# Pairs attention: two head groups worked as a pair, with 64-column quarters shared, and exponentials of three banks

## The chip, the core and the metric

The kernel runs on one core of one Trainium2 chip. The metric is the device time of one launch in microseconds, lower is better. Three timed runs of the kernel before gave 1415.05 us in the median (1402.74 to 1417.5). One more run was profiled; its own time is 1408.72 us and the span of its records is 1406.9 us.

## The reference

The program is a small vision tower: an embedding, and three layers with different attentions and feed-forward parts. The change is in the attention of the third layer's first half, called "pairs" in the kernel. It has 32 heads of width 2 over 1025 tokens, two batches, causal. Per head:

```python
q, k, v = split(x_normed @ w_qkv.T)            # heads of 2 values
q = rmsnorm(q) * qn_w ; k = rmsnorm(k) * kn_w
s = (q @ k.T) / sqrt(2)                        # causal: key <= query
y = softmax(s) @ v
x = x + y @ w_proj.T
```

The last token (number 1024) is treated apart, so the main loop works on 1024 tokens, which are 8 tiles of 128 keys by two halves of 512 queries.

## The kernel before, in words

`stage_pairs` is one stage of six. `pairs_prepare` (L2173) makes q, k and v; `pairs_attend` (L2334) does the attention; `pairs_project` (L2558) projects. In `pairs_attend`:

- Heads are worked four at a time. Two batches of 32 heads give `BH = 16` such head groups. The four heads of a group lie on partitions 0, 32, 64 and 96 (12 rows each, since q and k are split into bf16 parts that are multiplied exactly), so that their four score matmuls stand in different row strips of TensorE.
- A score block is 128 keys by 512 query columns of one head, one PSUM bank. The causal triangle makes 9 steps of four blocks (one per head) for each head group: `steps`. Step 0 is key tile 0 against queries 0 to 511; step 1 joins tile 1 (384 columns) with tile 3 (128 columns); step 2 joins 256 columns of the first query half with 256 of the second; steps 3 to 7 are whole tiles against queries 512 to 1023; step 8 joins tiles 5 and 7.
- TensorE computes the scores of a step (L2546), in two units of two banks each. PSUM has six banks for scores, so three units are in flight: a unit waits for the exponential of the unit three before it (`exp_ok`, `u - 2`).
- ScalarE exponentiates a unit (L2476), 128x1024 from PSUM into the ring `PT` in SBUF, which holds four steps.
- VectorE sets the part above the diagonal to zero (L2460): a multiplication with the triangle `keep` over 128 columns of four heads. That is 8 instructions for a head group: one in steps 0 and 7, two in steps 1, 2 and 8.
- TensorE then multiplies the weights with the values, in float32, two steps behind the scores (`attend(n - 2)`, L2512): four heads in four column strips, 32 columns of the array each, accumulating in PSUM bank 6. When a query half is complete, VectorE copies bank 6 to `Yc` (L2453, semaphore `y_sb`), and the first attend of the next half waits for that copy.
- Bank 7 is used by the "turns": four transposes that bring q or k of the next head group (L2501, copied by VectorE at L2418), and transposes that bring the result of the head group before back (L2492; L2406 and L2408 divide it). One turn stands behind each of steps 0 to 6.

TensorE's program is thus written by hand: for each step, scores, then the attend of two steps before, then a turn. All engines work in order. A wait in TensorE's program holds up all that stands behind it.

Of the kernel before, what the change touches and what calls it, by code (L numbers as in the profile page):

```python
# [21 lines left out]
D = 64  # L22
# [29 lines left out]
def constants():  # L52
# [48 lines left out]
    c["c_keep"] = np.triu(np.ones((128, 128), np.float32))  # L101
# [2056 lines left out]
def stage_pairs(nc, K, A):  # L2158
    with ExitStack() as ctx:
# [3 lines left out]
        V1 = sb("V1", [128, T, 128])  # L2163
        qk = sb("qk", [128, T, 128])
        wpT = sb("wpT", [64, 64])
        pairs_prepare(nc, K, A, Q12, K12, V1, qk, wpT)
        Yt = sb("Yt", [128, 16, 32, 2])
        YL = sb("YL", [1, 2, 32, 2])
        pairs_attend(nc, K, A, Q12, K12, V1, qk, Yt, YL)
# [3 lines left out]
def pairs_prepare(nc, K, A, Q12, K12, V1, qk, wpT):  # L2173

    with ExitStack() as ctx:
# [23 lines left out]
        with nc.Block() as block:  # L2199
# [7 lines left out]
            @block.gpsimd  # L2207
            def _(pool):
                nc.gpsimd.memset(zero[:], 0.0).then_inc(zero_ok, 1)
                nc.gpsimd.memset(V1[:], 1.0).then_inc(ones_ok, 1)  # L2210

# [101 lines left out]
            def _(pe):  # L2313
# [7 lines left out]
                for u in range(9):  # L2321
# [12 lines left out]
def pairs_attend(nc, K, A, Q12, K12, V1, qk, Yt, YL):  # L2334
# [3 lines left out]
    BH = 16  # L2338

    steps = [[(0, 0, 0, 0, 512)],  # L2340
             [(0, 1, 0, 128, 384), (0, 3, 384, 384, 128)],
             [(0, 2, 0, 256, 256), (1, 6, 256, 256, 256)]]
    steps += [[(1, j, 0, 0, 512)] for j in range(5)]
    steps += [[(1, 5, 0, 128, 384), (1, 7, 384, 384, 128)]]
    per = len(steps)
    diag = {0: (0,), 1: (0, 384), 2: (0, 256), 7: (0,), 8: (0, 384)}
    RING = 4
    N = BH * per

    TURNS = {0: ("q", 0), 1: ("q", 1), 2: ("k", 0), 3: ("k", 1), 4: ("y", 0), 5: ("y", 1), 6: ("y", 2)}  # L2350
    YTILES = ((0, 3), (3, 6), (6, 8))
    LAST_STEP = 4 * per + 8

    def turns_at(n):
        bh, s = n // per, n % per
        found = []
        if s in TURNS:
            which, i = TURNS[s]
            owner = bh - 1 if which == "y" else bh + 1
            if 0 <= owner < BH:  # L2360
                found.append((owner, which, i))
# [3 lines left out]

    FIRST = [(0, which, i) for which in "qk" for i in range(2)]
    number = {turn: k for k, turn in enumerate(FIRST + [turn for n in range(N + per) for turn in turns_at(n)])}
    masked = [0]
    for n in range(N):
        masked.append(masked[-1] + (n % per in diag))  # L2370
    with ExitStack() as ctx:
# [4 lines left out]
        keep = sb("keep", [128, 128])  # L2376
        QT = sb("QT", [128, 2, 1024], BF16)
        KT = sb("KT", [128, 2, 1024], BF16)
        PT = sb("PT", [128, RING, 4, 512])
# [8 lines left out]
        chain, ls_ok, le_ok, lw_ok = sem("chain"), sem("ls_ok"), sem("le_ok"), sem("lw_ok")  # L2388
        with nc.Block() as block:
            @block.sync  # L2390
            def _(sp):
                sp.dma_start(keep[:], A["c_keep"]).then_inc(c_in, 16)

            @block.vector
            def _(dve):
# [4 lines left out]
                def bring(bh, which, i):  # L2400
# [13 lines left out]
                    else:  # L2414
                        if bh >= 2:
                            dve.wait_ge(s_ps, 2 * per * (bh - 1))
                        dst = QT if which == "q" else KT
                        ins = nc.vector.tensor_copy(dst[:, bh % 2, 512 * i:512 * i + 512],  # L2418
                                                    ps[:, 7, :].bitcast(BF16)[:, 0:512])
# [21 lines left out]

                for t in FIRST:
                    bring(*t)
                dve.wait_ge(c_in, 16)
                for n in range(N + per):
                    bh, s = n // per, n % per
                    if n >= 2 and n - 2 < N and (n - 2) % per in (2, 8):
                        c = (n - 2) % per // 8
                        k = 2 * ((n - 2) // per) + c
                        dve.wait_ge(av_ps, n - 1)  # L2450
                        if k >= 4:
# [1281 lines left out]
```

## Time and profile before

| | |
|---|---|
| median of three runs | 1415.05 us (1402.74 to 1417.5) |
| profiled execution, its own time | 1408.72 us |
| its span | 1406.9 us |
| PE busy (matmuls) | 1082.8 us, 77% |
| DVE busy | 890.9 us, 63% |
| ACT busy | 764.2 us, 54% |
| POOL busy | 139.2 us, 10% |
| exponentials of the pairs attention (L2476) | 288, busy 266.1 us, first at 652.1, last start 919.4 |

PE is TensorE's matmul row, PEld its weight loads, DVE is VectorE, ACT ScalarE, POOL GpSimd. The stage that the change touches most lies between 646 and 926 us of the span. The rest of the kernel is the same before and after. A float32 matmul appears in the trace as two records (two passes), and so do its weight loads; a bf16 matmul is one record. The record of a matmul begins when it starts to stream and ends when the last result is out, so records of successive matmuls overlap. The time that TensorE needs for a piece of work is best read from the start of one group to the start of the next.

### The profile page before, as it was taken

The numbers are of one execution on the slowest core, as the hardware profiler recorded it, in microseconds if no ns is written. First come the engines' busy times: TensorE is split into PE (matmuls) and PEld (weight loads), VectorE is DVE, ScalarE is ACT, GpSimd is POOL, SyncE is SP. The second block draws the span as 40 slices with busy tenths as digits, with TensorE's granted clock in tenths as the row PEclk, the third lists the DMA queues.
The fourth block names the chain that finished last, engine by engine and source line by source line (L and its number), as shares of the span: only waits on it lengthen the run. The fifth ranks groups of instructions, "written<-read, shape, count | busy, mean of one in ns | idle before, by whom it ended". The sixth has DMA issues, their size and how long they took to land. (4 is left out here: it accounts for less than half of the span.)

```text
span 1406.9 us, 27739 instructions
## 1 busy us (share of the span) xinstructions
PE 1082.8 (77%) x11399; PEld 620.2 (44%) x11399; DVE 890.9 (63%) x1928; ACT 764.2 (54%) x1071; POOL 139.2 (10%) x163
## 2 busy tenths in 40 slices
PE   6667974562879869945999999989799999997240
PEld 3456963351534444431333333354555566665220
DVE  0476537967891177775675555454788998974524
ACT  0452322231207643358999999932488997982020
POOL 0005401410001200000000000010000000000524
PEclk9788975775659979976999999978899999998575
DMA  7100000021000000000000000010000000002021
GB/s 147 29 1 1 4 4 17 0 34 44 3 0 2 1 0 1 1 2 3 1 2 1 1 1 1 2 24 18 1 2 2 2 3 2 2 2 68 14 45 27
DMA packets 42740, 18.23 MB, mean 13 GB/s; under 512 B 37930, under 2 KB 41564, under 8 KB 42360
## 3 DMA queue, kind: packets, MB, share of 16 engines
q1 hardware_dynamic: 40888, 15.39, 5.2%
q0 software_dynamic: 1728, 1.08, 0.4%
q8 instruction: 91, 1.49, 0.4%
q14 instruction: 33, 0.27, 0.1%
HBM read 12.95 MB, written 3.48 MB: 12 GB/s over the span
## 5 line engine op out<-in xcount | busy, mean ns | idle before, releaser
L2476 ACT ACTIVATE pt_PT<-ps 128x1024 f32<-128x1024 f32 x288 | 266.1, 1108 | 5.9 <-PE ps L2546 5.6
L3459 DVE TENSOR_SCALAR da_AD<-da_QH,da_XG,da_XH 128x1024 f32<-128x1024 f32 x296 | 219.8, 808 | 29.8 <-PE ps L3588 28.8
L3507 ACT ACTIVATE da_AD<-ps,da_NX 128x1024 f32<-128x1024 f32 x214 | 221.2, 1132 | 30.4 <-PE ps L3588 29.9
L3588 PE MATMUL ps<-da_AD,dw_win 128*32 128x256 f32 x4080 | 227.6, 380 | 0.0
L3588 PEld LDWEIGHTS ps<-da_AD,dw_win 128*32 128x32 f32 x4080 | 129.8, 110 | 94.5 <-DVE da_AD L3459 9.7
L2512 PE MATMUL ps<-pt_PT,pa_V 128*32 128x512 f32 (+3 forms) x1536 | 155.5, 499 | 8.3 <-DVE pt_Yc L2453 3.2
L2460 DVE TENSOR_TENSOR pt_PT<-pt_PT,pt_keep 128x512 f32<-128x512 f32 x128 | 84.2, 689 | 61.3 <-ACT pt_PT L2476 60.2
L2546 PE MATMUL ps<-pt_QT,pt_KT 12*128 12x512 bf16 (+3 forms) x768 | 80.2, 334 | 3.2 <-DVE pt_KT L2418 0.5
L2512 PEld LDWEIGHTS ps<-pt_PT,pa_V 128*32 128x32 f32 x1536 | 38.9, 109 | 64.8 <-issue 63.6
L2085 ACT ACTIVATE mt_act<-ps 128x342 f32<-128x342 f32 (+1 forms) x66 | 30.1, 455 | 54.4 <-PE ps L2140 54.4
L2140 PE MATMUL ps<-mt_XF,ew_w 64*128 64x342 f32 (+1 forms) x132 | 54.6, 498 | 0.8 <-ACT mt_WT L2071 0.8
L2142 PE MATMUL ps<-mt_XF,ew_w 64*128 64x342 f32 (+1 forms) x132 | 53.5, 510 | 0.0
L1799 PE MATMUL ps<-gq_KT,gq_QT 128*114 128x342 bf16 (+2 forms) x144 | 44.5, 435 | 11.3 <-DVE gm_mx L1725 9.1
L2546 PEld LDWEIGHTS ps<-pt_QT,pt_KT 12*128 12x128 bf16 x768 | 22.6, 92 | 61.9 <-ACT pt_PT L2476 35.4
L1882 ACT ACTIVATE gt_PT<-ps 114x684 f32<-114x684 f32 (+2 forms) x72 | 42.5, 643 | 11.5 <-PE ps L1923 11.2
L2046 DVE TENSOR_TENSOR mt_prod<-ps,mt_act 128x342 f32<-128x342 f32 (+1 forms) x66 | 33.6, 509 | 16.4 <-ACT mt_act L2085 14.7
L707 ACT COPY rc_T<-ps 114x128 f32<-114x128 f32 (+1 forms) x54 | 14.1, 264 | 48.8 <-PE ps L625 47.8
L2051 DVE TENSOR_TENSOR mt_H<-ps,mt_prod 128x342 f32<-128x342 f32 (+1 forms) x66 | 33.9, 514 | 9.0 <-DVE mt_prod L2046 0.5
L2406 DVE RECIPROCAL pt_rec<-ps 128x12 f32<-128x12 f32 (+1 forms) x48 | 10.6, 220 | 43.7 <-PE ps L2492 43.7
L1865 DVE COPY gt_Y<-ps 128x342 f32<-128x342 f32 x6 | 3.1, 515 | 52.2 <-PE ps L1901 52.2
L1799 PEld LDWEIGHTS ps<-gq_KT,gq_QT 128*114 128x114 bf16 x144 | 20.5, 188 | 34.2 <-DVE gm_mx L1725 31.1
L1761 ACT COPY gq_QT<-ps 99x342 bf16<-99x342 bf16 x12 | 4.7, 454 | 56.3 <-PE ps L1809 55.6
(779 smaller groups left out, 2041.7 us busy)
## 6 DMA issues: line engine op xcount, KB each, us to landing
em_xs<-in_x_dram SPq DMA_DIRECT2D x2, 1152.0 KB, 9.3
em_xs<-in_x_dram SPq DMA_DIRECT2D x2, 1024.0 KB, 13.6
cp_xbuf<-ci_zero SPq DMA_DIRECT2D x1, 672.0 KB
cp_XS<-cp_xbuf SPq DMA_DIRECT2D x8, 84.0 KB, 2.2
cp_ybuf<-cp_YS SPq DMA_DIRECT2D x8, 84.0 KB, 2.1
ew_win<-in_L_ffn_w_dram SPq DMA_DIRECT2D x2, 320.0 KB
em_WS<-in_L_tok_W_dram SPq DMA_DIRECT2D x8, 72.0 KB
la_blk<-la_scratch SPq DMA_DIRECT2D x8, 64.1 KB
```

The source lines that it names most:

```text
L1799: ins = nc.tensor.matmul(ps[0:P, b0 + c, 0:w], QT[:, h, t * P:(t + 1) * P], KT[:, h // 2, k0:k0 + w], start=True, stop=True)
L1882: nc.scalar.activation(PT[:, n % 4, :, 0:w], ps[0:P, b0:b0 + 2, 0:w], ACT.Exp, scale=0.25).then_inc(exp_ok, 1)
L2051: tt(H[0:r, n % 4], ps[0:r, b0 + 2, 0:GRP], prod[0:r, n % 2], ALU.mult).then_inc(hid_ok, 1)
L2140: nc.tensor.matmul(ps[0:r, b0, 0:GRP], w13[0:64, 128 * c:128 * c + r], XF[0:64, cols], start=True, stop=True).then_inc(gate_ps, 1)
L2142: nc.tensor.matmul(ps[0:r, b0 + 1, 0:GRP], w13[64:128, 128 * c:128 * c + r], XF[64:128, cols], start=True, stop=True).then_inc(up_ps, 1)
L2460: ins = tt(d, d, bc(keep[:], 4), ALU.mult)
L2476: nc.scalar.activation(PT[:, n % RING, 2 * i:2 * i + 2, :], ps[:, b0:b0 + 2, :], ACT.Exp, scale=SCALE).then_inc(exp_ok, 1)
L2512: ins = nc.tensor.matmul(ps[32 * q:32 * q + 32, 6, q0:q0 + w], V1[:, (bh // 8) * 8 + j, v0:v0 + 32], PT[:, n % RING, q, p0:p0 + w], start= ...
L2546: ins = nc.tensor.matmul(ps[:, 2 * (u % 3) + q % 2, p0:p0 + w], KT[32 * q:32 * q + 12, bh % 2, j * 128:(j + 1) * 128], QT[32 * q:32 * q + ...
L3459: nc.vector.tensor_scalar(AD[:, j % RING], QH[:, b], XG[:, b, s:s + 1], XH[:, b, s:s + 1], ALU.max, ALU.subtract).then_inc(ad_dve, 1)
L3507: nc.scalar.activation(AD[:, j % RING], QA, ACT.Abs, bias=NX[:, b, s:s + 1]).then_inc(ad_act, 1)
L3588: ins = nc.tensor.matmul(o, D.win[:, int(by[j] == "D"), hp, 15 - m:47 - m], AD[:, j % RING, hp], start=False, stop=m == (14 if (k, q) == ( ...
```

## The change

Two head groups (an even one and an odd one) become a pair of 17 steps in place of 18. In each query half the last piece of the triangle (tile 3 of the half, 64 of its query columns, and the two diagonal 64x64 quarters) is taken out of the steps; the four such pieces of a pair (two head groups, two halves) fill one shared step, number 5 of the pair, called "X". Diagonal tiles are cut into 64-column quarters ("S"): keys 0 to 63 of one tile against 64 queries, and keys 64 to 127 of the neighbouring tile (there the halves of q's and v's rows are exchanged) against the next 64 queries, so that two half tiles stand above each other in one 64-column strip. Their value matmuls take `VZ`, a copy of v in which half of the rows is zero, one matmul for each tile.

So a step is now one of: four whole steps; `first` (two S quarters of 64 columns and 448 columns of tile 4c); `second` (192 and 320 columns); and in the shared step, per head, four times 64 columns of tile 3 and two S quarters.

The blocks of all steps but X run through units of three banks (`UNIT = 3`), with `SLOTS = 2` units in flight: a unit waits for the exponential of the unit two before it. X has two units of two banks. An exponential is 128x1536 (170 of them), 128x1024 for X (16) and once at the end. A pair has 64 blocks outside X, that is 21.33 units of three. The ring holds 18 blocks. Attends are run behind the unit in which the last block of a step stands (`last`), still two steps behind; X has no attend of its own, its pieces are added to the attends of the four `second` steps.

On VectorE the masks are 12 instructions of 512 elements for a pair in place of 16; q is copied by three instructions in place of one. GpSimd fills `VZ`. In `pairs_prepare` the qkv matmul of every second tile is cut in two of 64 rows.

```diff
+    UNIT, RING = 3, 18
+    SLOTS = 6 // UNIT
+    def first(c):
+        return [("S", c, 4 * c, 0, 0, 64), ("K", c, 4 * c, 64, 64, 448)]
+    def second(c):
+        return [("K", c, 4 * c + 2, 0, 320, 192), ("K", c, 4 * c + 1, 192, 192, 320)]
+    def rest(c, p0):
+        return [("K", c, 4 * c + 3, p0, 448, 64), ("S", c, 4 * c + 2, p0 + 64, 0, 64)]
+    whole = [[("K", 1, j, 0, 0, 512)] for j in range(4)]
+    ends = [first(1), second(1), first(0), second(0)]
+    SHARED, OPEN = 5, (0, 7, 9, 15)
+    duo = [(0, parts) for parts in whole + ends[:1]] + [(0, None)] + [(0, parts) for parts in ends[1:]]
+    duo += [(1, parts) for parts in whole + ends]
...
+            @block.gpsimd
+            def _(pool):
+                for r, i in ((slice(0, 64), 0), (slice(64, 128), 1)):
+                    nc.gpsimd.tensor_copy(VZ[r].rearrange("p (t i) c -> p t i c", i=2)[:, :, i],
...
+                            nc.vector.tensor_copy(to[:, :, 0], src[:, :, 0])
+                            for r in range(2):
+                                ins = nc.vector.tensor_copy(to[:, :, 1, r], src[:, :, 1, 1 - r])
...
+                    if kind == "X":
+                        for q in range(4):
+                            if q % 2 == 0:
+                                dve.wait_ge(exp_ok, last[n] + q // 2)
+                            d = PX[:, q].rearrange("p (r c) -> p r c", c=128)
+                            ins = tt(d, d, bc(keep[:, 0:128], 4), ALU.mult)
...
-                        nc.scalar.activation(PT[:, n % RING, 2 * i:2 * i + 2, :], ps[:, b0:b0 + 2, :], ACT.Exp,
-                                             scale=SCALE).then_inc(exp_ok, 1)
...
+                    nc.scalar.activation(to, ps[:, b0:b0 + k, :], ACT.Exp, scale=SCALE).then_inc(exp_ok, 1)
...
+                                    ops.append((o[0:64, p0:p0 + 64], kt[:, 128 * j:128 * j + 64],
+                                                qt[:, 128 * j:128 * j + 64]))
+                                    ops.append((o[64:128, p0:p0 + 64], kt[:, 128 * j + 192:128 * j + 256],
+                                                qt[:, 128 * j + 128:128 * j + 192]))
+                        work.append(ops)
+                    for x in range(max(len(ops) for ops in work)):
+                        for ops in work:
+                            if x < len(ops):
+                                out, keys, queries = ops[x]
+                                ins = nc.tensor.matmul(out, keys, queries, start=True, stop=True)
...
+                    if KIND.get(s) == "E":
+                        c = parts[0][1]
+                        ins = weigh(d * per + SHARED, rest(c, QUARTER[odd, c]), bh, False)
...
+                    if u >= SLOTS:
+                        pe.wait_ge(exp_ok, u - SLOTS + 1)
+                    scores(u)
+                    while step < N and last[step] == u:
+                        if step >= 2 and (step - 2) % per != SHARED:
+                            attend(step - 2)
+                        for t in turns_at(step):
+                            turn(*t)
+                        step += 1
...
-                        ins = nc.tensor.matmul(ps[:, (6 + u) % 8, 192 * i:192 * i + 192],
-                                               XT[:, c0:c0 + 128] if u < 8 else XL[:, i], WT[:], start=True, stop=True)
+                        if u < 8 and i:
+                            for r in (64, 0):
+                                ins = nc.tensor.matmul(o[64 - r:128 - r], XT[:, c0 + r:c0 + r + 64], WT[:], start=True,
+                                                       stop=True)
```

What TensorE runs at the start of a head group, before: steps 0 to 2 with their turns (`pt_QT,pt_KT` are scores, `pt_PT,pa_V` an attend, `pt_identb` a turn; the sizes are output rows by columns).

```order
L2546 MATMUL ps<-pt_QT,pt_KT 128x512 x4
L2512 MATMUL ps<-pt_PT,pa_V 32x512 x4
L2501 MATMUL ps<-pt_identb,pa_Q 128x128 x4
L2546 MATMUL ps<-pt_QT,pt_KT 128x384
L2546 MATMUL ps<-pt_QT,pt_KT 128x128
L2546 MATMUL ps<-pt_QT,pt_KT 128x384
L2546 MATMUL ps<-pt_QT,pt_KT 128x128
```

Every score matmul there has 128 output rows; only the number of columns varies.

After, the same engine in the second half of a pair: a unit of three `first` blocks, then a unit of one `first` block and two `second` blocks, an attend and a turn.

```order
L2621 MATMUL ps<-pt_QT,pt_KT 64x64 x6
L2621 MATMUL ps<-pt_QT,pt_KT 128x448 x3
L2621 MATMUL ps<-pt_QT,pt_KT 64x64
L2621 MATMUL ps<-pt_QT,pt_KT 128x192 x2
L2621 MATMUL ps<-pt_QT,pt_KT 64x64
L2621 MATMUL ps<-pt_QT,pt_KT 128x320 x2
L2621 MATMUL ps<-pt_QT,pt_KT 128x448
L2634 MATMUL ps<-pt_PT,pa_V 32x512 x4
L2578 MATMUL ps<-ident,pt_Yc 128x128 x3
```

Matmuls with 64 output rows now stand between those with 128. After, the same engine, one of the two units of the shared step X:

```order
L2621 MATMUL ps<-pt_QT,pt_KT 128x64 x2
L2621 MATMUL ps<-pt_QT,pt_KT 64x64 x4
L2621 MATMUL ps<-pt_QT,pt_KT 128x64 x2
L2621 MATMUL ps<-pt_QT,pt_KT 64x64 x4
L2621 MATMUL ps<-pt_QT,pt_KT 128x64 x2
L2621 MATMUL ps<-pt_QT,pt_KT 64x64 x4
L2621 MATMUL ps<-pt_QT,pt_KT 128x64 x2
L2621 MATMUL ps<-pt_QT,pt_KT 64x64 x4
```

Twenty-four small matmuls, the shape changing seven times inside the unit, fill two banks. And a `second` attend after, which carries the pieces of X behind its own:

```order
L2634 MATMUL ps<-pt_PT,pa_V 32x192 x4
L2634 MATMUL ps<-pt_PT,pa_V 32x320 x4
L2634 MATMUL ps<-pt_PX,pa_V 32x64 x4
L2634 MATMUL ps<-pt_PX,pa_VZ 32x64 x8
```

ScalarE, whose program before was 288 exponentials of 128x1024, has after (the second pair's X in the middle):

```order
L2563 ACTIVATE pt_PT<-ps 128x1536 x22
L2563 ACTIVATE pt_PX<-ps 128x1024 x2
L2563 ACTIVATE pt_PT<-ps 128x1536 x4
```

Fewer and longer exponentials, the short ones together in one place of each pair.

## Rows read from the trace of the kernel before

**Rows 1.** Busy time (x instructions) of PE, PEld, DVE, ACT, POOL; granted clock; DMA; GB/s

```profile
700.00:900.00 200.00, 193.36 (x2022) 66.51 (x2018) 115.89 (x250) 199.74 (x218) 0.00 (x0) 1.00 0.01 2
```

**Rows 2.** The page's costliest groups: exponentials; count, busy us, mean ns, idle before

```profile
L2476 ACT ACTIVATE pt_PT<-ps 128x1024 f32<-128x1024 f32 x288 | 266.1, 1108 | 5.9 <-PE ps L2546 5.6
```

**Rows 3.** Order of time, weight loads: start us, us, engine, line, tile, idle before

```profile
854.73 0.30 PEld L2546 LDWEIGHTS ps<-pt_QT,pt_KT 12*128 12x128 bf16 x8
855.39 0.19 PEld L2512 LDWEIGHTS ps<-pt_PT,pa_V 128*32 128x32 f32 x8 [0.36 <-issue]
...
856.42 0.23 PEld L2501 LDWEIGHTS ps<-pt_identb,pa_Q 128*128 128x128 bf16 x4 [0.20 <-issue]
856.75 0.13 PEld L2546 LDWEIGHTS ps<-pt_QT,pt_KT 12*128 12x128 bf16 x8
...
860.89 0.19 PEld L2512 LDWEIGHTS ps<-pt_PT,pa_V 128*32 128x32 f32 x8 [0.37 <-issue]
861.49 0.31 PEld L2492 LDWEIGHTS ps<-ident,pt_Yc 128*128 128x128 f32 x3 [0.41 <-DVE pt_KT L2418]
...
862.57 0.16 PEld L2512 LDWEIGHTS ps<-pt_PT,pa_V 128*32 128x32 f32 x8 [0.23 <-issue]
...
864.00 0.31 PEld L2492 LDWEIGHTS ps<-ident,pt_Yc 128*128 128x128 f32 x3 [0.41 <-issue]
864.48 0.10 PEld L2546 LDWEIGHTS ps<-pt_QT,pt_KT 12*128 12x128 bf16 x4 [0.17 <-issue]
864.80 0.16 PEld L2512 LDWEIGHTS ps<-pt_PT,pa_V 128*32 128x32 f32 x8 [0.23 <-issue]
865.80 0.20 PEld L2492 LDWEIGHTS ps<-ident,pt_Yc 128*128 128x128 f32 x2 [0.84 <-DVE pa_Yt L2408]
866.17 0.10 PEld L2546 LDWEIGHTS ps<-pt_QT,pt_KT 12*128 12x128 bf16 x4 [0.17 <-ACT pt_PT L2476]
```

**Rows 4.** The same for matmuls: an attend that waits for VectorE's copy

```profile
857.39 1.06 PE L2512 MATMUL ps<-pt_PT,pa_V 128*32 128x512 f32 x8 [0.23 <-DVE pt_Yc L2453]
```

**Rows 5.** Who waited for whom, 700 to 900 us: total us, times, longest

```profile
PEld ps L2546 <- ACT pt_PT L2476: 22.6, 60, 0.8
```

**Rows 6.** Groups by form over the span, ScalarE: count, busy us, mean ns

```profile
L3482 ACT ACTIVATE da_PP<-ps 128x1024 f32<-128x1024 f32 x8 | 8.4, 1049 | 7.6 <-PE ps L3588 7.6
L2269 ACT COPY pa_Q<-pp_zero 128x5120 f32<-128x5120 f32 x1 | 4.5, 4460 | 1.7 <-POOL pp_zero L2209 1.7
```

**Rows 7.** Order of time, matmuls of an earlier stage: rows*columns of the array

```profile
192.81 0.36 PE L773 MATMUL ps<-rc_M,rw_TM 114*64 114x114 f32 x4
193.10 0.41 PE L773 MATMUL ps<-rc_R,rc_M 64*64 64x114 f32 x4
...
195.29 0.34 PE L784 MATMUL ps<-rw_BK,rc_UZ 114*64 114x64 f32 x4
195.45 0.29 PE L786 MATMUL ps<-rc_UZ,rw_BK 114*64 114x64 f32 x4
195.57 0.29 PE L789 MATMUL ps<-rw_TM,rw_BK 114*64 114x64 f32 x4
195.69 0.37 PE L792 MATMUL ps<-rc_M,rc_UZ 114*64 114x114 f32 x4
```

**Rows 8.** Groups by form, 700 to 900 us: score matmuls

```profile
L2546 PE MATMUL ps<-pt_QT,pt_KT 12*128 12x512 bf16 x288 | 36.3, 385 | 1.3
L2546 PE MATMUL ps<-pt_QT,pt_KT 12*128 12x384 bf16 x96 | 14.4, 332 | 0.0
```

**Rows 9.** The same view, VectorE: mask, copy of bank 6, copy of q

```profile
L2460 DVE TENSOR_TENSOR pt_PT<-pt_PT,pt_keep 128x512 f32<-128x512 f32 x96 | 63.1, 689 | 40.4 <-ACT pt_PT L2476 39.4
L2453 DVE COPY pt_Yc<-ps 128x512 f32<-128x512 f32 x24 | 16.6, 691 | 6.6 <-PE ps L2512 6.1
L2418 DVE COPY pt_QT<-ps 128x512 bf16<-128x512 bf16 x24 | 10.0, 415 | 0.0
```

**Rows 10.** Order of time in pairs_prepare: TensorE's qkv matmuls

```profile
616.26 5.46 PE L2329 MATMUL ps<-pp_WT,pp_XT 64*128 64x192 f32 x32
```

More of the change, by code:

```diff
@@ L2505, in turn, with scores @@
                     ins.then_inc(turn_ps, 1)
-                def weigh(n, parts, start, stop):
-                    bh = n // per
-                    for k, (c, j, p0, q0, w) in enumerate(parts):
-                        for q in range(4):
-                            v0 = 3 * (4 * (bh % 8) + q)
-                            ins = nc.tensor.matmul(ps[32 * q:32 * q + 32, 6, q0:q0 + w],
-                                                   V1[:, (bh // 8) * 8 + j, v0:v0 + 32],
-                                                   PT[:, n % RING, q, p0:p0 + w], start=start and k == 0,
-                                                   stop=stop and k == len(parts) - 1, skip_group_check=True)
+                def scores(u):
+                    blocks = units[u]
+                    work = []
+                    for k, (n, q) in enumerate(blocks):
+                        d, s = divmod(n, per)
+                        o = ps[:, UNIT * (u % SLOTS) + k]
+                        odd, parts = duo[s]
+                        sets = [(odd, parts)]
+                        if s == SHARED:
+                            sets = [(i, rest(c, QUARTER[i, c])) for i in range(2) for c in (1, 0)]
+                        rows = slice(32 * q, 32 * q + 12)
+                        ops = []
+                        for i, some in sets:
+                            kt, qt = KT[rows, i], QT[rows, i]
+                            for kind, c, j, p0, q0, w in some:
+                                if kind == "K":
+                                    ops.append((o[:, p0:p0 + w], kt[:, 128 * j:128 * j + 128],
+                                                qt[:, 512 * c + q0:512 * c + q0 + w]))
+                                else:
+                                    ops.append((o[0:64, p0:p0 + 64], kt[:, 128 * j:128 * j + 64],
[8 more added lines that the diff above has]
+                                ins = nc.tensor.matmul(out, keys, queries, start=True, stop=True)
+                    ins.then_inc(s_ps, 1)
@@ new lines, in weigh @@
+                def weigh(n, parts, bh, start):
+                    for k, (kind, c, j, p0, q0, w) in enumerate(parts):
+                        tile = (bh // 8) * 8 + j
+                        if kind == "K":
+                            cases = [(V1, tile, q0, w)]
+                        else:
+                            cases = [(VZ, tile, 128 * (j - 4 * c), 64), (VZ, tile + 1, 128 * (j + 1 - 4 * c), 64)]
+                        for src, t, to, width in cases:
+                            for q in range(4):
+                                v0 = 3 * (4 * (bh % 8) + q)
+                                ins = nc.tensor.matmul(ps[32 * q:32 * q + 32, 6, to:to + width],
+                                                       src[:, t, v0:v0 + 32], weights(n, q)[:, p0:p0 + width],
+                                                       start=start and k == 0, stop=False, skip_group_check=True)
```

219 lines of the change are left out of this document (130 added, 89 removed).

## The prediction

> **What bounds the kernel now.** I read first the share of each engine over the middle of the stage, then the lines of the exponentials, then who waited for whom, and last the order of time of TensorE over one head group, because the change rewrites that order. Between 700 and 900 us ScalarE is busy 199.74 of 200 us, TensorE's matmul row 193.36, and the granted clock is 1.00, that is 2.4 GHz [rows 1]. The 288 exponentials have 266.1 us of busy time and hardly any idle time before them [rows 2]: ScalarE paces the stage, one 128x1024 exponential in 266.1 / 288 = 0.924 us. A head group has 18 of them, 16.63 us.
>
> TensorE is close behind, and that is what matters here. Its waits for exponentials are 22.6 us in 200, so 1.9 in 16.63 [rows 5], part of it only in the weight loads. Its own work for a head group, from start to start in [rows 3]: an attend of 512 columns 1.00 (864.80 to 865.80), one of 384 + 128 columns 1.03, of 256 columns 0.60, of 512 + 256 columns 1.43; scores of four blocks 0.33 (864.48 to 864.80; the rows of 864.00 to 866.17 show one step and its turns), cut in two pieces 0.66 with a short wait in it (854.73 to 855.39), I take 0.6; a turn of q or k 0.33, of the result 0.48, 0.48 and 0.37. Nine steps are 5 x 1.00 + 2 x 1.03 + 0.60 + 1.43 = 9.1 of attends, 6 x 0.33 + 3 x 0.6 = 3.8 of scores and 4 x 0.33 + 1.33 = 2.65 of turns: 15.5 of 16.63 us. For two head groups it is 31.0 of work under 33.26 us of exponentials. So only 7% lies between the two engines.
>
> **ScalarE's side of the change.** A 128x5120 copy takes 4460 ns and a 128x1024 exponential that nothing overlaps 1049 ns: 3411 / 4096 = 0.833 ns a column [rows 6]. Of the 0.924 us, 0.853 is columns and 0.071 fixed. A 128x1536 exponential then follows the last after 1.280 + 0.071 = 1.351 us. A pair has 21.33 of them and two of 0.924: 30.7 us in place of 33.26. Eight pairs would save 20.5 us, 15 of it by the step that is gone and 5.5 by fewer instructions. The Trainium skill (ScalarE: Activation LUTs, What ACT_TABLE_LOAD costs) gives 186 ns + 0.833 a column with 93 ns overlapped when they follow each other, so 0.946 and 1.373 us, an estimate; the trace's 0.924 decides, and by the page the gain would be the same within 1 us.
>
> **TensorE's side.** I went through the second pair's units in the new order and priced each by the rows above.
>
> Attends: eight whole ones 8.0; four `first` ones of 448 + 64 + 64 columns; four `second` ones with the pieces of X, 192 + 320 + 3 x 64 columns. A 64-column float32 group costs 0.12 where it follows its like (L789 to L792, 195.57 to 195.69 [rows 7]), against 0.107 by columns (0.43 for 256 [rows 3]). So 1.15 and 1.38, in sum 8.0 + 4.6 + 5.5 = 18.1, as much as before (18.2).
>
> Scores: 13 units of plain pieces, nine followed by an attend (0.33) and four followed by another unit (0.25), 4.0. Three blocks now stream side by side where four did, so whole blocks alone take 21.33 units, where 18 groups did before. The rest holds the 64-row quarters. Each time the shape of the matmul changes, the array runs empty first: L773 with 114 rows streams two passes of 114 columns, 0.19 us, but the next L773, with 64 rows, starts 0.29 later (192.81 to 193.10), while matmuls of one shape follow without it (L786 to L789 to L792) [rows 7]. That is 0.10 us a change. In the new order the shape changes 19 times inside the eight units that hold `first` blocks and 14 times in the two units of X. With 0.05 for a short piece, 0.19 for 448 columns (512 against 384 columns differ by 53 ns [rows 8], 0.41 ns a column) and 0.12 at the end, the eight units are 0.79, 0.46, 0.97, 0.75, 0.79, 0.75, 0.36, 0.74 = 5.6 us, and X is 1.15 + 1.24 = 2.4. Scores are 4.0 + 5.6 + 2.4 = 12.0 against 7.6. X's exponentials are 1.85 us, so X alone is slower on TensorE than on ScalarE.
>
> The rule behind it: the Trainium skill (TensorEngine Tiling (Array Packing), Key Properties) says that changing the tiling mode, not only the tile, drains TensorE. The trace shows it for other shapes; that it also holds between 64 and 128 output rows at 12 input rows no row shows. With the rule the 33 changes cost 3.3 us a pair, without it none.
>
> Turns are unchanged, 5.3. TensorE's work for a pair is 18.1 + 12.0 + 5.3 = 35.4 us, above the 30.7 of the exponentials and above today's 33.26: TensorE becomes the bound.
>
> **Waits that come on top.** The first attend of a query half waits for the copy of bank 6, 0.69 us [rows 9], with a wait of 0.23 today [rows 4]. After the change the stretch between the two attends is a unit of 0.33 and sometimes a turn of 0.33; I find about 0.3 at one and 0.6 at another of the four places of a pair, 1.0 us in all. Behind that attend stand the next scores, and for those ScalarE waits. The masks: 12 of 0.69 us in place of 16 [rows 9], but four of them in a row for X, 2.8 us, with the result's division and the next mask behind; where TensorE is late anyway they are done in time, so 0. The two-unit depth: a unit may start only when the exponential two before is over, and it must be in PSUM 1.35 us later; while TensorE is the late one it seldom waits for that, so 0 to 0.3, I take 0. q's three copies in place of one (0.42 us [rows 9], at most 0.3 more) lie beside TensorE's attends; without that cover 64 of them would cost some 10 us at most, but VectorE is busy only 116 of 200 us [rows 1].
>
> A pair then takes 35.4 + 1.0 = 36.4 us, 3.1 more than 33.26; eight pairs 25 us. Before the loop, the qkv matmuls of `pairs_prepare` take 5.46 us for eight units, some 0.66 each [rows 10]; cut in two with two changes of shape it takes 0.2 to 0.3 more each, and VectorE's work starts after three of them: 0.8 us. GpSimd's new fill of `VZ` and its copy have VectorE's and ScalarE's whole preparation and the first four steps as cover: 0; without it, the copy would cost once what a stage of that size takes, 1 to 2 us.
>
> **Sum.** 1408.7 + 25.0 + 0.8 = 1434.5, say 1435 us. It is made against the profiled execution's 1408.72 us, which lies 0.4% under the median 1415.05 of the three runs, and inside their spread; against the median the same step gives 1441.
>
> **Bounds of the unknown costs.** Shape changes: 0 (no drain for these shapes) to 0.15 each (a drain and a weight load that nothing hides, as L784's 0.16 for a group that costs L789 0.12 [rows 7]): 32.1 to 37.0 us of work. 64-column float32 groups: 0.107 to 0.17 with four column strips, up to +1.0. Waits: 0.3 to 2.5. So a pair lies between 32.4 and 40 us.
>
> **Rivals.**
> (a) The shapes do not drain the array. TensorE's work is 35.4 - 3.3 = 32.1, with 1.0 of waits 33.1, today's 33.26. Time 1408, nothing won. For it: no row has these shapes. Against: every change of rows or columns that I found in the trace has the 0.10.
> (b) ScalarE stays the bound, the change does what its shape promises: 1408.7 - 20.5 = 1388, or up to 1402 where TensorE lags a little. It decides only if TensorE's work falls under 31 us, which needs (a), no waits, and cheap small matmuls too. For it: TensorE's row is mostly overlapping records, so my start-to-start prices may be pessimistic. Against: 93% use today, and 128 more small matmuls a pair.
> (c) The waits grow. With two units in flight a late unit is at once an idle ScalarE, and in five of eight pairs the attends of two steps fall behind one unit next to X, with X's four masks in front of the next attend's mask; 2 us more a pair, with small groups at 0.17: 1450 to 1475. For it: before, three units and a lead of a whole ring evened out the steps. Against: VectorE has 42% free.
>
> **Numbers.** The forecast, TensorE as the bound with drains, 1424 to 1450: 0.62. (a), within 1%: 0.17. (b) 0.12. (c) 0.09. The range 1406 to 1458 holds the forecast, most of (a) and the lower part of (c). About 1% is what a measurement of this kernel can tell from no change, so slower by more than 1% (over 1423) 0.70, within 1% 0.18, faster 0.12.
>
> **What the profile after would show.** Right: ScalarE busy about 245 us in L2563 but with 30 to 50 us of idle time before it, released by the scores; first to last exponential some 292 us against 267; TensorE's rows hardly ever waiting for ScalarE; 0.10 us gaps at each change between 64 and 128 output rows; the unit of X over 1.1 us from start to start. Wrong: idle time before L2563 under 10 us, an X unit of 0.5 us, or 128x1536 exponentials that follow each other by much more than 1.35 us. The forecast also fails if the attends with 64-column pieces cost well over 1.4 us, on the slow side.

## The result: 50 us slower, twice the forecast

The changed kernel takes 1464.94 us (median of four runs, 1461.41 to 1467.91); the kernel before, run beside it, 1414.64 us (1402.74 to 1417.5). The ratio is 1.0376, with a 95% interval of 1.0339 to 1.0413. The direction was forecast, the size (1435 us, at most 1458) was not. The profiled execution took 1463.91 us, its span is 1462.2 us, 55.3 more than before.

The page after, first the granted clock in 40 slices of the span (slices 18 to 27 are the stage), then the exponentials, the attends and the scores (count, busy us, mean ns, idle before):

```profile
PEclk9888977757579699757998989886899999999565
...
L2563 ACT ACTIVATE pt_PT<-ps 128x1536 f32<-128x1536 f32 x171 | 239.2, 1449 | 63.6 <-PE ps L2621 62.6
...
L2634 PE MATMUL ps<-pt_PT,pa_V 128*32 128x512 f32 (+3 forms) x1280 | 151.3, 570 | 8.5 <-DVE pt_Yc L2537 6.7
L2621 PE MATMUL ps<-pt_QT,pt_KT 12*64 12x64 bf16 (+5 forms) x1280 | 111.6, 291 | 7.5 <-ACT pt_PT L2563 4.7
```

ScalarE has 239.2 us of these and 16.4 of X's 16 exponentials, 255.6 in place of 266.1 [rows 2], but 63.6 us of idle time before the long ones where it had 5.9, nearly all of it ended by the scores. The same stretch as in [rows 1], and who waited for whom in it:

```profile
700.00:900.00 200.00, 191.39 (x2659) 84.84 (x2660) 89.98 (x238) 161.38 (x120) 0.00 (x0) 0.91 0.01 2
```

```profile
ACT pt_PT L2563 <- PE ps L2621: 33.9, 43, 3.6
...
PE ps L2634 <- DVE pt_Yc L2537: 4.1, 10, 1.3
...
PE ps L2621 <- ACT pt_PT L2563: 2.6, 5, 0.8
```

TensorE is the late engine, as forecast: it is busy 191 of 200 us and waits for exponentials 2.6 us, while ScalarE waits for it 33.9. New is the column after the busy times: the granted clock is 0.91 where it was 1.00. The two rows below are windows from the first exponential's start to the last one's end (the loop, its ends taken to within 0.3 us), of the kernel before and of the changed one:

```profile
652.10:920.50 268.40, 258.78 (x2646) 87.18 (x2645) 150.82 (x322) 266.46 (x289) 0.00 (x0) 0.98 0.01 1
```

```profile
649.50:972.40 322.90, 308.18 (x4134) 133.86 (x4132) 136.07 (x359) 255.34 (x188) 0.00 (x0) 0.87 0.01 2
```

The loop grew by 54.5 us of the span's 55.3, so it holds nearly the whole difference. The trace's clock records say when TensorE ran at 1.2 GHz: 8.4 us of the loop before, all at its start, and 81.8 us after, in the start and in nine later stretches of 3.4 to 13.7 us. One of these, as three windows:

```profile
736.00:741.50 5.50, 5.18 (x67) 2.11 (x65) 3.11 (x8) 5.13 (x4) 0.00 (x0) 1.00 0.00 1
741.50:748.40 6.90, 6.53 (x54) 2.17 (x50) 4.05 (x5) 3.67 (x4) 0.00 (x0) 0.51 0.01 2
748.40:760.00 11.60, 10.58 (x184) 5.46 (x187) 6.11 (x19) 9.04 (x7) 0.00 (x0) 1.00 0.01 1
```

And TensorE's weight loads around it, in order of time (start us, us, ..., count, idle before):

```profile
739.80 0.26 PEld L2621 LDWEIGHTS ps<-pt_QT,pt_KT 12*64 12x64 bf16 x9
740.39 1.10 PEld L2621 LDWEIGHTS ps<-pt_QT,pt_KT 12*128 12x128 bf16 x24 [0.33 <-DVE pt_KT L2476]
741.94 1.63 PEld L2621 LDWEIGHTS ps<-pt_QT,pt_KT 12*128 12x128 bf16 x27 [0.45 <-issue]
743.74 0.29 PEld L2621 LDWEIGHTS ps<-pt_QT,pt_KT 12*64 12x64 bf16 x4 [0.17 <-issue]
744.41 0.20 PEld L2634 LDWEIGHTS ps<-pt_PT,pa_V 128*32 128x32 f32 x8 [0.38 <-issue]
745.27 0.20 PEld L2634 LDWEIGHTS ps<-pt_PT,pa_V 128*32 128x32 f32 x4 [0.66 <-ACT pt_PX L2563]
746.12 0.20 PEld L2634 LDWEIGHTS ps<-pt_PT,pa_V 128*32 128x32 f32 x4 [0.66 <-issue]
747.98 0.10 PEld L2621 LDWEIGHTS ps<-pt_QT,pt_KT 12*128 12x128 bf16 x2 [1.66 <-issue]
```

The two units of the shared step X begin at 740.39, the clock falls at 741.5, the second unit takes 1.80 us (741.94 to 743.74) where 1.24 was forecast, and the attends that follow run at half speed (745.27 to 746.12 is 0.85 us for four loads and their matmuls, which take 0.43 at full clock, 779.85 to 780.28 in e6 below). Each of the seven later X has a fall that begins 1 to 4 us after its first matmul. The first X (659.2) lies in the half-clock start of the stage, and the clock falls again 11 us later; the ninth fall follows an earlier one by 3.4 us.

**An account of the 54.5 us.** A stretch at 1.2 GHz does half its work, so it costs at most half its length. (81.8 - 8.4) / 2 = 36.7 us, an upper bound; the rest is 17.8 us. I call this second part the remainder: what the loop lost at full clock, at the least. The forecast had 25 for the remainder and nothing for the clock.

### The profile page after: what moved, and what is told of

Read it like the earlier page. It is cut to its first block and busy times, and to the rows that moved or that the text cites. A ratio compares the mean times of both kernels' runs of the same rounds, so it can differ in the third digit from the quotient of the medians.

```text
span 1462.2 us, 30850 instructions
## 1 busy us (share of the span) xinstructions
PE 1136.0 (78%) x12951; PEld 662.8 (45%) x12951; DVE 877.7 (60%) x1968; ACT 753.7 (52%) x970; POOL 142.9 (10%) x166
## 5 line engine op out<-in xcount | busy, mean ns | idle before, releaser
L2563 ACT ACTIVATE pt_PT<-ps 128x1536 f32<-128x1536 f32 x171 | 239.2, 1449 | 63.6 <-PE ps L2621 62.6
L3631 ACT ACTIVATE da_AD<-ps,da_NX 128x1024 f32<-128x1024 f32 x214 | 221.3, 1132 | 30.7 <-PE ps L3712 30.1
L2634 PE MATMUL ps<-pt_PT,pa_V 128*32 128x512 f32 (+3 forms) x1280 | 151.3, 570 | 8.5 <-DVE pt_Yc L2537 6.7
L2621 PE MATMUL ps<-pt_QT,pt_KT 12*64 12x64 bf16 (+5 forms) x1280 | 111.6, 291 | 7.5 <-ACT pt_PT L2563 4.7
L2621 PEld LDWEIGHTS ps<-pt_QT,pt_KT 12*128 12x128 bf16 (+1 forms) x1280 | 45.3, 98 | 64.2 <-issue 32.0
L2634 PEld LDWEIGHTS ps<-pt_PT,pa_V 128*32 128x32 f32 x1280 | 32.0, 116 | 50.3 <-issue 38.8
L2519 DVE TENSOR_TENSOR pt_PT<-pt_PT,pt_keep 128x512 f32<-128x512 f32 (+1 forms) x36 | 22.3, 629 | 34.8 <-ACT pt_PT L2563 34.4
L2537 DVE COPY pt_Yc<-ps 128x512 f32<-128x512 f32 x32 | 22.1, 691 | 34.0 <-PE ps L2634 34.0
L2476 DVE COPY pt_KT<-ps 128x512 bf16<-128x512 bf16 x32 | 13.6, 425 | 44.1 <-PE ps L2589 44.1
L708 ACT COPY rc_T<-ps 114x128 f32<-114x128 f32 (+1 forms) x54 | 14.1, 264 | 48.3 <-PE ps L626 47.3
L1800 PEld LDWEIGHTS ps<-gq_KT,gq_QT 128*114 128x114 bf16 x144 | 20.5, 188 | 34.1 <-DVE gm_mx L1726 31.0
```

Source lines behind the costliest of these rows:

```text
L1800: ins = nc.tensor.matmul(ps[0:P, b0 + c, 0:w], QT[:, h, t * P:(t + 1) * P], KT[:, h // 2, k0:k0 + w], start=True, stop=True)
L2563: nc.scalar.activation(to, ps[:, b0:b0 + k, :], ACT.Exp, scale=SCALE).then_inc(exp_ok, 1)
L2621: ins = nc.tensor.matmul(out, keys, queries, start=True, stop=True)
L2634: ins = nc.tensor.matmul(ps[32 * q:32 * q + 32, 6, to:to + width], src[:, t, v0:v0 + 32], weights(n, q)[:, p0:p0 + width], start=start and ...
L3631: nc.scalar.activation(AD[:, j % RING], QA, ACT.Abs, bias=NX[:, b, s:s + 1]).then_inc(ad_act, 1)
```

## The experiments

The first question was whether the shape changes of X make the clock fall, or the sharing, or the two-unit depth. All runs in one table. "Half" is the time at 1.2 GHz in the loop, "falls" the stretches of it that begin after the stage's start; remainder = loop - 268.4 - (half - 8.4) / 2. "Idle" is the exponentials' idle time in the page's costliest row; in the runs with a shared step X's own 16 exponentials are not in it (e8's have 30.6 us more). Loop, half, falls and idle come from one profile of each kernel, the time and the ratio from 4 to 10 executions. The start of the stage, before any fall, has 7 to 21 us at 1.2 GHz from profile to profile (17 in after, e3 and e4, 7 in e2 and e7), so differences of 10 us in "half" can come from there. Ratios are to the kernel before beside the same run.

| Run | time us | ratio (95%) | loop | half (falls) | remainder | idle |
|---|---|---|---|---|---|---|
| before | 1414.64 | | 268.4 | 8.4 (0) | 0 | 5.9 |
| after | 1464.94 | 1.0376 (1.0339-1.0413) | 322.9 | 81.8 (9) | 17.8 | 63.6 |
| e1_units3 | 1414.09 | 1.0023 (0.9998-1.0049) | 276.0 | 10.8 (0) | 6.4 | 18.0 |
| e11_two_two | 1431.72 | 1.0157 (1.0118-1.0197) | 296.1 | 10.9 (0) | 26.4 | 27.0 |
| e2_share | 1437.02 | 1.0172 (1.0121-1.0224) | 292.3 | 41.5 (7) | 7.3 | 31.1 |
| e3_rows128 | 1437.15 | 1.0176 (1.0138-1.0214) | 287.1 | 41.2 (6) | 2.3 | 39.2 |
| e4_grouped | 1434.22 | 1.0182 (1.0135-1.0230) | 291.4 | 41.1 (5) | 6.6 | 42.6 |
| e7_grouped2 | 1419.52 | 1.0048 (1.0023-1.0074) | 267.5 | 7.0 (0) | -0.2 | 15.1 |
| e9_zero2 | 1407.74 | 0.9988 (0.9966-1.0011) | 262.0 | 13.3 (1) | -8.8 | 13.3 |
| e5_smalls | 1436.43 | 1.0152 (1.0108-1.0197) | 295.7 | 34.7 (6) | 14.1 | 31.1 |
| e6_smalls128 | 1412.13 | 1.0002 (0.9978-1.0026) | 270.4 | 7.4 (0) | 2.5 | 7.9 |
| e8_filler | 1489.24 | 1.0531 (1.0477-1.0586) | 343.3 | 95.8 (8) | 31.2 | 61.9 |
| e10_fill_full | 1467.24 | 1.0434 (1.0376-1.0491) | 318.3 | 30.7 (1) | 38.8 | 42.2 |
| e12_smalls_two | 1419.48 | 1.0061 (1.0026-1.0096) | 282.0 | 17.7 (0) | 8.9 | 23.9 |

**The larger exponentials alone.** e1 is the kernel before with units of three banks, two in flight, nothing shared:

```
-    for i in range(2): ... activation(PT[:, n % RING, 2*i:2*i+2], ps[:, b0:b0+2], Exp)
+    for u, blocks in enumerate(units):
+        activation(PT[:, g % RING:g % RING + k], ps[:, b0:b0+k], Exp)
```

> The kernel before with units of three banks and two in flight, and nothing shared: the other half of the change alone. Theory A (TensorE's extra work in the 64-row quarters, and a TensorE clock that falls at each shared step X, are the loss): without quarters TensorE's work for two head groups stays near 31.5 us, ScalarE needs 24 x 1.351 = 32.4 us in place of 33.26, the clock stays at 1.00 in the stage, so 1403 to 1412 us. Theory B (two units in flight is what costs, a late unit is at once an idle ScalarE): 1430 us or more, with the idle time before the exponentials that the changed kernel has.

```profile
L2484 ACT ACTIVATE pt_PT<-ps 128x1536 f32<-128x1536 f32 x192 | 261.7, 1472 | 18.0 <-PE ps L2554 18.0
```

ScalarE's busy time falls by 4.4 us (7 were priced: 266 against 192 x 1.351 = 259), and 12 us more of idle time take it back. The expectation missed, if by little. So this half of the change is worth nothing here even with TensorE's work unchanged.

**The depth alone.** e11 is the program of e1 with units of two banks and still only two in flight. Against the kernel before it also has e1's ring of 18 blocks in place of 16.

```
-    UNIT, RING = 3, 18
-    SLOTS = 6 // UNIT
+    UNIT, RING = 2, 18
+    SLOTS = 2
```

> The kernel before with two units of two banks in flight where it has three: nothing is shared, nothing enlarged, only the depth goes from three to two. If the depth costs what the run with units of three banks left unexplained (6.5 us saved in the exponentials, nothing in the time), the exponentials' idle time grows from 8 us by 8 us or more and the time is 1420 to 1435 us, clock 1.00. If the depth costs nothing, 1412 to 1416 us, and the loss in the run with units of three banks was in the larger units themselves.

1431.72 us, clock 1.00 between 700 and 900 us: the depth is no free parameter, it costs 28 us of loop at 1024 columns; with units of 1536 columns (e1), whose longer exponentials give a little back, the loop is 7.6 us longer. I read it so: after an attend of 1.00 and scores of 0.33 the next scores must be there before the unit in ScalarE ends, and 1.351 us covers that, 0.924 doesn't; that reading is an argument and was not tried further.

**The sharing alone.** e2 is the changed kernel with units of two banks, three in flight (`UNIT = 2`).

> The changed kernel with units of two banks and three in flight: the sharing alone. Theory A: nearly as slow as the changed kernel, 1445 to 1465 us, the clock at half for several us at each X. Theory B: three units even out the steps, and a step in eighteen is saved: 1400 to 1415 us.

Better than expected by 8 us, but 1.7% slower than before with 272 exponentials in place of 288. The clock falls seven times.

**The changes of shape.** e3 is the changed kernel in which the quarters' scores are matmuls of 128 output rows, which changes what is computed: half of those scores come from the wrong keys, and the amount of work and its order stay. e4 keeps the right scores and sorts the matmuls of a unit by shape.

```
 e3: -  ops.append((o[0:64, p0:p0 + 64], kt[:, 128*j:128*j + 64], ...))
     +  ops.append((o[:, p0:p0 + 64], kt[:, 128*j:128*j + 128], ...))
 e4: +  for rows in (64, 128):
     +      same = [[o for o in ops if o[0].shape[0] == rows] for ops in work]
```

> The changed kernel, but each 64-row score matmul of a quarter writes 128 rows (same count, same columns; the upper or lower half of those scores is then of the wrong keys). No change of shape is left among the scores. Theory A: 33 changes of 0.10 us a pair go, 3.3 us, so 26 us less: 1439 us if the clock still falls at X, about 1415 if it does not. If changes of shape cost nothing (the first rival of the prediction): 1460 to 1470, as the changed kernel.

> The changed kernel with the score matmuls of a unit sorted by shape, all with 64 rows first, then all with 128: X's units have one change in place of seven, the others one or none. Theory A: some 22 changes less a pair, 2.2 us, 18 us in all: 1447 us if the clock still falls at X, 1425 to 1430 if it does not. If changes cost nothing: 1460 to 1470.

Both gain about 2% and stop there. e3 was forecast at 1439 if the clock still falls and came out at 1437; e4, forecast at 1447, came out 13 us lower, since half of the time at 1.2 GHz went too. At full clock the loss falls from 17.8 to 2.3 and 6.6 us, about or below the 6.4 that units of three banks cost in e1, so the larger part of the remainder went with the changes of shape. But half the time at 1.2 GHz stays, in e3 with no change of shape in the scores at all. So the shapes are one cause of the falls and not the only one.

e7 sorts the shapes and has three units in flight:

> The changed kernel with score matmuls sorted by shape and units of two banks, three in flight. Sorting alone gave back 28 us and units of two alone 28 us. If both do it by keeping the clock up (half of the stage's half-clock time went in each), together they save the rest of the clock, not twice 28: 1410 to 1420 us, with under 20 us at half clock in the loop. If each takes away a stall of its own, 1405 to 1410.

No fall is left, and the time is within the forecast 1410 to 1420. Of the four kernels (sorted or not, two or three in flight) the time at half clock is 81.8, 41.1, 41.5 and 7.0 us: each of the two properties adds 34 us by itself, and both add 75. Counted without the start of the stage it is 64.8, 23.9, 34.1 and 0.

**Only small matmuls, in the kernel before.** e5 puts 24 small score matmuls, cycling through 128, 64 and 64 output rows, ahead of each of two units in every second head group; the real scores write over them. In e6 all have 128 rows.

```
+  for x in range(12):
+      for k in range(2):
+          matmul(ps[rows[x % 3], 2*(u % 3) + k, c0:c0+64], KT[strip, ...], QT[strip, ...])
```

> The kernel before, with the 24 small score matmuls of an X unit (8 of 128x64, 16 of 64x64, the shape changing seven times) put ahead of each of the two units of one step in every second head group; what they write is overwritten by the real scores. It is the cost of X alone: 2.1 us of TensorE's time for two head groups, where 2.3 are free. Theory A (such a stretch also makes the TensorE clock fall for several us): half-clock stretches begin within some us of these matmuls, and the time goes to 1425 to 1440 us. Without an effect on the clock: the clock stays at 1.00 in the stage and three units in flight absorb it, 1410 to 1416 us.

> As the last, but all 24 matmuls with 128 rows, so without changes of shape: about 1 us for two head groups. Theory A: less idle array, the clock falls seldom or never: 1408 to 1414 us. If small matmuls as such, not the changes of shape, make the clock fall: as the last one.

This is the cleanest pair: same kernel, same count, same columns, and only the rows differ. Windows of e5 about one of its bursts:

```profile
770.00:777.00 7.00, 6.56 (x88) 2.85 (x87) 5.97 (x12) 7.00 (x9) 0.00 (x0) 1.00 0.01 2
777.00:780.00 3.00, 3.00 (x55) 1.79 (x53) 0.89 (x3) 2.39 (x3) 0.00 (x0) 1.00 0.00 0
780.00:783.40 3.40, 3.40 (x21) 1.10 (x19) 0.00 (x0) 1.02 (x1) 0.00 (x0) 0.50 0.02 5
783.40:790.00 6.60, 6.48 (x56) 1.46 (x54) 1.84 (x6) 5.99 (x7) 0.00 (x0) 1.00 0.00 0
```

The matmul row is busy 3.00 of 3.00 us in the burst, and the clock falls right behind it: busy in this row is not what holds the clock. Counted from their first matmul to the work behind them the bursts of e5 take 2.5 to 2.7 us, those of e6 0.65 (its first 1.0), and e6 costs nothing and loses no clock. Six of e5's eight bursts have a fall that begins 1.7 to 4 us after their first matmul, two have none. The pair also tests the account above: the longer bursts are 14.6 us in all, the clock (34.7 - 7.4) / 2 = 13.7, together 28.3 where the loop grew by 25.3. So halving the time at 1.2 GHz gives the right size, some 3 us too much here.

**Filler in the changed kernel.** If the array is idle during the drains, other matmuls might hold the clock. e8 adds four matmuls of 12 input rows, 512 columns, to each unit of X, into the free bank; e10 the same four with 128 input rows:

```
 e8:  +  matmul(ps[:, free], KT[64:76, 0, 0:128], QT[64:76, 0, 0:512])
 e10: +  matmul(ps[:, free], identb[:], QT[:, 0, 0:512])
```

> The changed kernel, with four matmuls of 128x512 more behind the small ones of each X unit, into the bank that X leaves free: 0.9 us of work more for a unit, 1.7 us a pair, 14 us in all, and the array busy in that stretch. If the fall of the clock is what costs half of the loss, and an idle array at X is what brings it: the half-clock time of the loop goes from 82 to under 45 us and the time comes to 1440 to 1455 us in spite of the added work. If the clock does not depend on it: 1475 to 1482 us.

> The changed kernel with four extra 128x512 matmuls of 128 input rows (bf16, an identity as weights, into the free bank) a unit that holds diagonal quarters: as many and as long as the filler matmuls of 12 input rows that left the clock where it was (1489 us, 93 us at half). Theory A2 (the work the array does counts, so a stretch of full-height matmuls holds the clock): half-clock time in the loop under 50 us, granted clock of the stage 0.93 or more, time 1440 to 1460 us in spite of the extra 7 to 14 us of TensorE work. Theory A1 (the changes of shape let it fall whatever stands beside them): like the run with filler of 12 rows, 80 to 100 us at half, time 1475 to 1495 us.

Windows of e8 and of e10:

```profile
700.00:900.00 200.00, 192.66 (x2529) 83.00 (x2522) 85.08 (x224) 149.14 (x110) 0.00 (x0) 0.88 0.01 2
```

```profile
700.00:900.00 200.00, 191.62 (x2699) 85.45 (x2698) 90.69 (x241) 161.81 (x119) 0.00 (x0) 0.97 0.01 2
```

The thin filler holds nothing (95.8 us at half; the 93 in the expectation of e10 leaves out the last 8 us of the loop), and 1489 us is above even the 1475 to 1482 expected for no effect. The full-height one takes the falls from nine to one, although it adds changes of shape. So changes of shape do not by themselves let the clock go, and a busy matmul row does not hold it; of two fillers that keep the row busy alike, only the one that works on the whole height of the array kept the clock. Their weights differ too (keys in e8, an identity in e10), and that was not tried apart. The time of e10 is still 1467 us, above the expected 1440 to 1460, since the filler costs TensorE 64 x 0.217 = 13.9 us and its own changes of shape (two at each of 16 units, 3 us), and TensorE is the bound; 38.8 - 17 leaves 22, near the 17.8 of the changed kernel. It is a probe, not a cure.

The Trainium skill (TensorE: Matmul & The Clock Gate, Part 1) says that TensorE's clock is set by how busy the engine has been. The pair e8 and e10 agrees only if that busyness is not the busy share of the profile's matmul row, which is 96% in both.

**The same scores without changes of shape.** e9 has the sharing, two banks and three in flight, and computes each quarter as two accumulating 128-row matmuls against a second copy of the keys in which the other tile's 64 keys are zero:

```
-  ops.append((o[0:64, p0:p0+64], kt[:, 128*j:128*j+64], ...))
-  ops.append((o[64:128, p0:p0+64], kt[:, 128*j+192:128*j+256], ...))
+  ops.append((o[:, p0:p0+64], kz[:, 128*j:128*j+128], ..., start=True, stop=False))
+  ops.append((o[:, p0:p0+64], kz[:, 128*j+128:128*j+256], ..., start=False, stop=True))
```

> The diagonal quarters still share 64 columns, but every score matmul has 128 output rows: a quarter is two accumulating matmuls against two copies of the keys, in each of which the other tile's 64 keys are zero, so the sums are right and no shape changes. Units are two banks (128x1024) with three in flight, as before. Theory A (the clock falls where the score stretch keeps changing shape): granted clock 1.00 in the stage as in the run with small matmuls of 128 rows (half-clock time in the loop about 7 to 11 us), the bursts that hold diagonal quarters under 1.1 us a unit; exponentials 256 x about 1.035 us less overlap = 243 us busy, idle 15 to 25 us, time 1404 to 1415 us, against 1419.5 for the shape-sorted run. Rival C (what lets the clock fall is the mask, copy or wait pattern of a shared unit, not its shapes): clock below 0.97, over 25 us at half, time 1425 to 1440 us.

```profile
L2569 ACT ACTIVATE pt_PT<-ps 128x1024 f32<-128x1024 f32 x256 | 240.8, 1081 | 13.3 <-PE ps L2627 11.8
```

```profile
700.00:900.00 200.00, 187.44 (x3266) 84.21 (x3264) 115.88 (x338) 196.10 (x211) 0.00 (x0) 1.00 0.01 2
```

1407.74 us against 1408.22 of the kernel before beside it: the whole loss is gone, with 13.3 us at half where 7 to 11 were expected. The loop is 6.4 us shorter than before, but the time is the same within the interval. The loop began 6.6 us later in its profile (658.7 against 652.1); over all profiles the start lies between 647.6 and 658.7 us, on average at 652.3 in the six with the old preparation and at 654.6 in the eight with the new one, so perhaps 2 us of it belong to the longer preparation, and I can't tell more. Behind the loop the eight take 3 us more on average as well (489.6 against 486.4 us to the end of the span), which no run here explains. e7, with a loop no longer than before, has its 0.5% there and in a start 5.7 us later. No version that beats the kernel before came out of this.

**Thin bursts with two in flight.** What e3 and e4 have beside shapes: is it depth two with thin matmuls? e12 is e1 with the 48 small matmuls of e6.

> The run with units of three banks and two in flight (1414 us, nothing shared, 10.8 us at half clock in the loop), with the 48 small matmuls of 128 output rows put ahead of one step in every second head group, whose results the real scores write over. With three units in flight those small matmuls cost nothing (1412 us, clock 1.00). Theory D (with two in flight, any stretch of thin matmuls lets the clock fall, which would explain the 41 us at half in the two runs of three-bank units with whole-height or shape-sorted shared units): over 20 us at half clock in the loop, granted clock of the stage 0.98 or less, time 1422 to 1440 us. Theory D0 (depth two and thin full-height matmuls do no harm together, so the 41 us have another cause in the shared units, their short pairs of exponentials): under 15 us at half, clock 1.00, time 1414 to 1420 us.

No fall after the start of the stage (the 17.7 us, which lie between the two forecasts, are its first ones, 650.4 to 668.0), so this explanation fails on the clock, while the time is 0.4% above e1's.

The traces of e3 and e4 show what else stands before their falls. In the changed kernel, in e2 and in e5 most falls come right behind small matmuls that change shape, with the matmul row busy nearly throughout. In e3 and e4 TensorE had stood idle for part of the time: in e4's X for the exponentials that free its banks (first fence, the fall is at 846.9), and before e3's fall at 732.1, 10 us ahead of an X, because an attend waited 1.75 us for its exponential (second fence).

```profile
844.55 0.54 PE L2623 MATMUL ps<-pt_QT,pt_KT 12*64 12x64 bf16 x24 [1.04 <-ACT pt_PT L2563]
845.37 0.54 PE L2623 MATMUL ps<-pt_QT,pt_KT 12*64 12x64 bf16 x7 [0.29 <-ACT pt_PX L2563]
```

```profile
728.70:732.10 3.40, 1.65 (x43) 0.76 (x33) 2.75 (x7) 2.17 (x2) 0.00 (x0) 1.00 0.02 5
```

e12's bursts have no such wait (3.39 of 3.40 us busy, 765.0 to 768.4). So waits with only two units in flight are the likely second cause. That is read from the traces and not shown by a run: e7 has one wait as long (1.66 of 3.40 us busy, 723.2 to 726.6) and keeps its clock. The two short exponentials of X in a row, which bring such waits, were not tried by themselves.

## Why the prediction was right in direction and wrong in size

**ScalarE's side: right within 5%.** Busy 255.6 us, forecast "about 245". An exponential that comes after a wait takes longer than one behind another, 1049 against 924 ns in [rows 6] and [rows 2]; the forecast had priced idle time and full overlap together.

**TensorE's prices at full clock: right within some per cent.** Weight loads of the changed kernel where the clock was full:

```profile
703.12 2.24 PEld L2621 LDWEIGHTS ps<-pt_QT,pt_KT 12*128 12x128 bf16 x48 [0.84 <-issue]
705.40 0.16 PEld L2634 LDWEIGHTS ps<-pt_PT,pa_V 128*32 128x32 f32 x8
...
722.45 0.57 PEld L2621 LDWEIGHTS ps<-pt_QT,pt_KT 12*64 12x64 bf16 x8
723.22 0.16 PEld L2634 LDWEIGHTS ps<-pt_PT,pa_V 128*32 128x32 f32 x8 [0.20 <-issue]
...
727.72 0.16 PEld L2634 LDWEIGHTS ps<-pt_PT,pa_V 128*32 128x32 f32 x8 [0.20 <-issue]
728.12 0.13 PEld L2634 LDWEIGHTS ps<-pt_PT,pa_VZ 128*32 128x32 f32 x4 [0.24 <-issue]
728.50 0.24 PEld L2634 LDWEIGHTS ps<-pt_PT,pa_VZ 128*32 128x32 f32 x12 [0.24 <-issue]
728.83 0.20 PEld L2578 LDWEIGHTS ps<-ident,pt_Yc 128*128 128x128 f32 x2
729.20 0.11 PEld L2621 LDWEIGHTS ps<-pt_QT,pt_KT 12*128 12x128 bf16 x5 [0.17 <-issue]
729.53 0.48 PEld L2634 LDWEIGHTS ps<-pt_PT,pa_V 128*32 128x32 f32 x16 [0.21 <-issue]
730.15 0.40 PEld L2634 LDWEIGHTS ps<-pt_PX,pa_V 128*32 128x32 f32 x8
730.47 0.30 PEld L2634 LDWEIGHTS ps<-pt_PX,pa_VZ 128*32 128x32 f32 x16
730.86 0.10 PEld L2621 LDWEIGHTS ps<-pt_QT,pt_KT 12*128 12x128 bf16 x3
```

From start to start: X's two units 2.28 us (forecast 2.4), a unit with a `first` block 0.77 (0.75), its attend 1.11 (1.15), the `second` attend with X's pieces 1.33 (1.38).

**The drain of 0.10 us: right, for these shapes too.** In the single records a 64-column matmul of 64 rows is followed by one of 128 rows 0.144 us later, where e6's, all of one shape, stand 0.029 us apart, so 0.115 us a change; from 128 to 64 rows it is 0.128 behind 64 columns, and 0.314 behind 512 where its like follows after 0.217, so 0.10. That agrees with the rule of the Trainium skill (TensorEngine Tiling (Array Packing), Key Properties) that the prediction leaned on, and settles rival (a): it did not happen. Without the changes (e3) the remainder is 2.3 us in place of 17.8. This 15.5 is below the 26 that 33 changes a pair make (8 x 3.3), I think because the loop then stands on another floor, such as the 6.4 us of e1; no run shows it.

**Waits: right place, the depth priced too low.** The attends waited 4.1 us in 200 for the copy of bank 6, 0.8 a pair (forecast 1.0), VectorE's masks and its other copies cost little that is visible (90 of 200 us busy). "0 to 0.3, I take 0" for two units in flight was too low: after and e2 differ by the depth and the size of the unit that goes with it, 17.8 against 7.3 us at full clock, 1.3 us a pair, and further in the clock. e1 and e11 show the price outside the sharing.

**The step that failed: the clock.** The working read the granted clock of 1.00 in [rows 1] and priced every new instruction at it. No term and no rival asked whether the new mix of instructions would keep it. What the runs show in its place is a granted clock of 0.87 over the loop, 81.8 us of it at 1.2 GHz where there were 8.4: up to 36.7 of the 54.5 us, more than the forecast's whole loss. Everything at full clock came to 17.8 us or a little more against 25 forecast, so the sum without the clock was rather pessimistic. The direction was no luck, since TensorE's extra work and waits alone made the kernel slower; that the 25 came so near the 17.8 is partly luck, for the changes of shape gave less than priced (15.5 against 26) and the depth more (10.5 against 0). In e7 no fall is left and in e9 one of 3.4 us, and there the loss was 0.5% and nothing. Rival (c)'s band, 1450 to 1475, holds the result, but its mechanism (2 us more of waits a pair) has some 10 us in it, the price of depth two. And the forecast that "ScalarE idle 30 to 50 us, loop 292" measured 63.6 and 322.9: the marks named for it were right in kind, and the missing one was the PEclk column.

**The preparation: 0.8 us forecast, not resolved.** The start of the loop scatters by 11 us from profile to profile; in the changed kernel's own it began 2.9 us earlier than before.

## What to carry to other kernels

Before pricing a change on an engine whose clock can be granted or withheld, ask of each new stretch what it does to the clock, not only how long it is: here a 2.3 us stretch of thin matmuls that keep changing shape was followed by 3.4 to 13.7 us at half speed, and TensorE was the late engine. Keep the shape of neighbouring matmuls, even at the price of more of them (e9 against e2: whole-height matmuls on a zeroed copy in place of small ones won back 1.8%). And work saved on one of two engines that are 7% apart is worth at most that margin, while depth given up for larger instructions has a price of its own (7.6 us of loop here, 28 where the instructions stayed small).

## What the runs showed of the hardware that I had not expected

- The granted clock fell to 0.50 straight after 3.00 us in which the matmul row was busy 3.00 us (e5).
- Going from 64 to 128 output rows at 12 input rows, or back, takes TensorE 0.10 to 0.115 us each time.
- Four extra 512-column matmuls a unit of X with 12 input rows left 95.8 us at half clock (81.8 without them), with 128 input rows 30.7, of which 10.2 us after the stage's start.
- Sorting shapes and having three units in flight each took 40 us at half clock away, and together nearly all (81.8, 41.1, 41.5, 7.0).
- Exponentials of 1536 columns are worth less than priced: 192 of them have 261.7 us of busy time where 288 of 1024 have 266.1, so 50% more columns save 1.7%, too little to pay for any loss of depth.
